# One output-projection unit moved up in a group's first head, and the last logits placed ahead of the last projection's eviction

## What is computed

```python
xn = layernorm(x)
# attention: 32 query heads, 8 key/value heads of 128 channels
q, k, v = xn @ Wq.T, xn @ Wk.T, xn @ Wv.T          # split into heads
q, k = rmsnorm(q, q_norm_w), rmsnorm(k, k_norm_w)
scores = q @ k.T / sqrt(128) + where(rel > 0, -1e30, slope[head] * rel)
out = softmax(scores) @ v
s = out @ Wo.T
# feed-forward with 4-bit style weights (w - zero) * scale
g = silu((silu(xn @ gate) * (xn @ up)) @ down)
result = x + s * g
```

## Time and profile before

| | |
|---|---|
| median of 3 runs | 1325.37 us (1324.14 to 1325.52) |
| the profiled execution | 1325.52 us, of which span of the trace 1323.4 us |
| granted TensorE clock | 0.993 of full speed over the span |
| TensorE busy | 1287.3 us, 97% |
| VectorE busy | 970.1 us, 73% |
| GpSimd busy | 710.2 us, 54% |
| ScalarE busy | 649.8 us, 49% |

### The profile page before, as it was taken

How to read it: one execution, slowest core, us unless ns; L and a number is a source line. 1 busy time by engine, 2 the same in 40 slices (tenths; PEclk the granted TensorE clock), 3 DMA queues, 4 the chain that set the end, 5 groups by cost and what they waited for, 6 DMA issues and landing times. The chain is left out here.

```text
span 1323.4 us, 20983 instructions
## 1 busy us (share of the span) xinstructions
PE 1287.3 (97%) x7138; PEld 1105.0 (83%) x7138; DVE 970.1 (73%) x2072; ACT 649.8 (49%) x1422; POOL 710.2 (54%) x755
## 2 busy tenths in 40 slices
PE   7899999999999999999999999999999989999997
PEld 6778888888888888888888888888888878888886
DVE  4678787778777877787778777877788855555556
ACT  3555565556555555555555555555565523222222
POOL 8645464546455545554555455545555625555553
PEclk8899999999999999999999999999999999999999
DMA  3000000000000000100000000000020036455441
GB/s 121 17 17 17 33 17 17 17 32 17 17 17 32 17 17 17 33 17 17 17 33 17 17 16 33 17 17 17 17 64 20 5 77 194 128 127 127 127 127 64
DMA packets 29468, 57.88 MB, mean 44 GB/s; under 512 B 3648, under 2 KB 3648, under 8 KB 29248
## 3 DMA queue, kind: packets, MB, share of 16 engines
q1 hardware_dynamic: 29232, 56.16, 14.9%
q10 hardware_dynamic: 144, 0.52, 0.1%
HBM read 54.57 MB, written 2.10 MB: 43 GB/s over the span
## 5 line engine op out<-in xcount | busy, mean ns | idle before, releaser
L396 POOL TENSOR_TENSOR pb<-rel,coef 128x1024 f32<-128x1024 f32 (+7 forms) x256 | 293.7, 1162 | 123.9 <-PE T L907 118.1
L497 ACT ACTIVATE pb<-pb,low 128x1024 f32<-128x1024 f32 (+7 forms) x256 | 198.9, 777 | 188.6 <-DVE low L687 186.9
L487 ACT ACTIVATE pt_h<-T 128x512 fp32r<-128x512 f32 (+3 forms) x384 | 185.9, 486 | 115.0 <-PE T L907 111.6
L671 DVE TENSOR_TENSOR pt_l<-T,pt_h 128x512 fp32r<-128x512 f32 (+3 forms) x384 | 210.4, 551 | 41.2 <-ACT pt_h L487 41.1
L687 DVE CUSTOM_DVE_ANT_0 pb<-S,pb,ninv 128x1024 f32<-128x1024 f32 (+7 forms) x256 | 207.8, 812 | 40.7 <-PE S L929 35.8
L907 PE MATMUL T<-ident,pb 128*128 128x128 f32 x1152 | 190.7, 275 | 14.9 <-DVE pb L696 8.4
L907 PEld LDWEIGHTS T<-ident,pb 128*128 128x128 f32 x1152 | 141.6, 141 | 53.6 <-issue 14.0
L696 DVE TENSOR_SCALAR pb<-pb,rinv 128x1024 f32<-128x1024 f32 (+7 forms) x256 | 172.5, 674 | 9.0
L926 PE MATMUL S<-kT_h,q_h 128*128 128x512 f32 (+2 forms) x384 | 142.0, 370 | 0.0
L945 PE MATMUL O<-pt_h,v_h 128*128 128x512 f32 (+2 forms) x384 | 140.7, 366 | 1.0 <-DVE pt_l L671 1.0
L373 POOL TENSOR_TENSOR inv<-ms,cst 128x4 f32<-128x4 f32 x64 | 76.2, 1191 | 120.8 <-DVE ms L719 120.8
(11 more groups left out here) (148 smaller groups left out, 2898.7 us busy)
## 6 DMA issues: line engine op xcount, KB each, us to landing
wq_in<-in_wq SPq DMA_DIRECT2D x32, 256.0 KB, 2.8
wo_in<-in_wo SPq DMA_DIRECT2D x32, 256.0 KB, 2.6
stage<-in_wkv SPq DMA_DIRECT2D x7, 512.0 KB, 3.9
stage<-in_gate_w SPq DMA_DIRECT2D x14, 256.0 KB, 2.6
stage<-in_gate_z SPq DMA_DIRECT2D x14, 256.0 KB, 3.6
stage<-in_gate_s SPq DMA_DIRECT2D x14, 256.0 KB, 5.2
stage<-in_up_w SPq DMA_DIRECT2D x14, 256.0 KB, 5.3
stage<-in_up_z SPq DMA_DIRECT2D x14, 256.0 KB, 6.4
```

Source lines behind the costliest of these rows:

```text
L396: g_.tensor_tensor(pbuf(idx, t), rel[:, TOK - w:TOK], coef[:, t:t + 1].to_broadcast([P, w]), ALU.mult).then_inc(bias_ready, 1)
L487: a_.activation(pt_lot(pt_h, t, n), bank[:, 0:m * P].rearrange("p (k w) -> p k w", w=P), ACT.Copy).then_inc(tr_hi, 1)
L497: a_.activation(pbuf(idx, t), pbuf(idx, t), ACT.Exp, bias=low[:, idx:idx + 1], scale=-1.0, accum_out=rsum[:, idx:idx + 1]).then_inc(exps_r ...
L671: v_.tensor_tensor(pt_lot(pt_l, t, n), bank[:, 0:m * P].rearrange("p (k w) -> p k w", w=P), f(pt_lot(pt_h, t, n)), ALU.subtract).then_inc( ...
```

## The change

Two things, both only in the order of work; no instruction is added or taken away.

1. In the first head of groups 1 to 7, unit `w1_0` is made right behind scores 0 and scores 1, ahead of `v0_0`, and no longer between lots (6,0) and (6,1). Its eviction on DVE moves from behind the `pt_l` of lot (6,0) to behind the second normalise, ahead of `v0_0`'s low part. The wait that belongs to it now asks for all evictions up to the head before's `v1_3`.
2. In every head that has units, DVE takes the logits of the last tile (idx 7) before the eviction of `w3`, no longer after it.

```diff
@@ group_order
-        out += [f"qc0_{j}"] + [f"v0_{j}"] * prev + [f"w0_{j}", f"w1_{j}"] * w
+        if j == 0 and not first:
+            out += ["qc0_0", "w1_0", "v0_0", "w0_0"]
+        else:
+            out += [f"qc0_{j}"] + [f"v0_{j}"] * prev + [f"w0_{j}", f"w1_{j}"] * w
@@ vector, group
                 normalise(h, 1)
+                early = j == 0 and kind != "first"
+                if early:
+                    project(at, f"w1_{j}", unit + 1)
                 if prev:
                     v_lo(at, f"v0_{j}", (j - 1) % PER)
...
                 lot(h, 6, 0)
-                if w:
+                if w and not early:
                     project(at, f"w1_{j}", unit + 1, kind == "first")
                 lot(h, 6, 1)
...
                 v_lo(at, f"v1_{j}", j)
+                logits(h, 7)
                 if w:
                     project(at, f"w3_{j}", unit + 3, kind == "first")
-                logits(h, 7)
@@ tensor, group
                     project(at, f"w{n}_{j}", 4 * (j % 2) + n, h - 2 - j % 2, 0 if j >= 2 else 2,
-                            at.n(f"v0_{j - j % 2}"))
+                            at.a - 1 if early and n == 1 else at.n(f"v0_{j - j % 2}"))
...
                 if j == 0:
                     scores(h, 1)
+                if early:
+                    w_unit(1)
...
                 w_unit(0)
                 lot(h, 6, 0)
-                w_unit(1)
+                if not early:
+                    w_unit(1)
                 lot(h, 6, 1)
```

More of the change, by code:

```diff
@@ L1049, in group, with w_unit @@
                 prev = not (kind == "first" and j == 0)
-                def w_unit(n, h=h, j=j):
+                early = j == 0 and kind != "first"
+                def w_unit(n, h=h, j=j, early=early):
                     if kind == "first" and j < 2:
```

## The result

The changed kernel takes 1330.62 us (median of 6 runs, 1330.4 to 1331.82), the kernel before 1325.07 us in the runs beside it (1324.08 to 1325.52). The ratio is 1.0047 with a 95% interval from 1.0037 to 1.0058: slower by 5.55 us between the medians. The forecast was 1330.5, in a range from 1328 to 1334.7.

A forecast was written before the change was run, and what follows sets the result against it. TensorE, busy 97% of the span, was taken as the bound, with DVE as full in the first heads. 1325.4 + 5.1 (4.7 for groups 1 to 6, 0.4 for group 7, edit 2 nothing) = 1330.5 us, range 1328 to 1334.7.

The forecast's parts named there:

- The stall and what it is worth: TensorE before tile 7's T's, first heads of groups 1 to 7: 0.72 us a group, 5.0 us at most.
- Step A: DVE in front of ssum: the squares come late, so DVE idles 0.74 us and everything behind is late.
- Step B: On DVE, w1_0's eviction, 0.60 us, now stands in front of v0_0's low part and every pt_l.
- The three waits: New TensorE waits for DVE in front of w0_0 (0.58 us), lot (6,1) (0.4) and lot (5,0) (0.70).
- the two rivals in which DVE's lag does not reach it: At lot (5,0): intended gain alone, 1320.4 us, chance 0.07; only the wait at w0_0 counts, 1324.4 us, chance 0.08.
- The sum for a group: TensorE leaves lot (5,0) 0.79 us later in each of groups 1 to 6, 4.7 us in all.
- Group 7: The 0.40 us bracket before tile 3's T's takes up part of the lag; 0.4 us taken as remaining.
- The rule against the trace: Second normalise after the squares falls into POOL's power; the skill's exclusion rule was set aside and nothing added.
- the rival at 1334.7: The normalise waits for POOL's power to end, up to 0.6 us more in each of 7 groups; chance 0.10.
- step C: Named only in the experiments: scores 2 come later and the moved unit no longer covers the chain to lot (5,0).
- third place: Lot (5,0) on TensorE: needs the pt_l of lot (6,0), starts at 314.53, new wait 0.70 us.

The follow-up runs named there:

- e6: Kernel before, with three of w1_0's six matmuls and the squares' transposes ahead of v0_0, which takes qc0_0's output tile, in early heads; 1320.98 us, ratio 0.9974.
- e4: Changed kernel with the squares' transposes of a group's first head behind v0_0's third matmul, not its ninth; 1326.56 us, ratio 1.0013.
- e3: Changed kernel with w1_0's eviction in the first head of groups 1 to 7 cut from 512 to 8 columns; 1327.58 us, ratio 1.0024.
- e5: Changed kernel with the squares' transposes behind v0_0's third matmul and w1_0's eviction cut to 8 columns; 1324.93 us, ratio 1.0004.
- e1: Changed kernel with the last logits put back behind w3's eviction, leaving only the move of w1_0 and its eviction; 1330.41 us, ratio 1.0045.
- e8: From e6: all of w1_0 but 32 columns of its last matmul goes ahead of v0_0, eviction stays late; 1324.63 us, ratio 1.0001 to before.

## Why the prediction was right, point by point

**The stall and what it is worth.** Right. The bracket is gone in all seven heads. "7 x 0.72 = 5.0 us is the most that edit 1 can win" was never tested by itself; e6 wins 0.40 a group of it.

**Step A**, DVE idle 0.74 in front of `ssum`. The bracket is 0.66, and e4, which removes it, wins 0.73. The distance from squares to `ssum` was read as 0.64 and is 307.02 - 306.38 = 0.64. Counted from the k transposes `ssum` comes 10.19 us after and came 9.41 before, 0.78 later where the prediction had 0.74.

**Step B**, 0.60 for the eviction. From 308.61 to 309.21 it is 0.60; e3 removes 0.53 of it and wins 0.55.

**The three waits.** All at their place, for the reasons given. Predicted 0.58, 0.4 and 0.70; the first and the last have brackets of 0.51 and 0.52. That column counts from the modelled end of the last matmul and not from when the next could have started, so it reads less than the delay. In distances of starts the first is 309.02 to 310.04, 1.02 against 0.35 without a wait (e5, 438.69 to 439.04), and the last 313.11 to 314.10, 0.99 against 0.30 (before, 313.44 to 313.74). The three are then 0.67, about 0.25 and 0.69. Lot (5,0) starts 314.10 - 306.38 = 7.72 us behind the squares, where 7.62 was forecast and less than 7 would have been wrong; with that the two rivals in which DVE's lag does not reach it fall.

**The sum for a group.** Mis-sized: 0.79 predicted, 0.95 measured. The chain on DVE was right to 0.01: `ssum` to the `pt_l` of lot (6,0) is 313.27 - 307.02 = 6.25, and the prediction had 5.64 + 0.60. What was missing:

- The step from DVE's end to TensorE's start. I took 0.06, from the normalise and the T's behind it. Behind a low part it is 0.15: 309.21 + 0.68 = 309.89 to 310.04 at `w0_0`. At lot (5,0) that adds 0.09. It could have been read before: in the earlier trace rows the low part ends at 309.08 and `w0_0` starts at 309.23, a wait of a few hundredths that shows no bracket.
- From the k transposes to the squares it is 9.55 after (296.83 to 306.38) and 8.12 before (297.40 to 305.52), 1.43 more where I had 1.39 for the unit: 0.04.
- T's behind a wait take 0.38 to the next row (314.10 to 314.48) and 0.35 without one: 0.03.

0.79 + 0.09 + 0.04 + 0.03 = 0.95. The kinds of wait were right; the step mis-sized most is the one from DVE to TensorE.

**Group 7.** Wrong. I let 0.4 of the lag fall into the bracket in front of tile 3's T's. It is still there:

```profile
978.96 0.63 PE L913 MATMUL T<-ident,pb 128*128 128x128 f32 x4 [0.43 <-DVE pt_l L674]
```

and what holds it is seen in DVE's row for the logits of idx 4 in that head:

```profile
975.43 0.75 DVE L690 CUSTOM_DVE_ANT_0 pb<-S,pb,ninv 128x512 f32<-128x512 f32 x1 [1.12 <-PE S L935]
```

DVE waits there for TensorE's own scores, so the chain in front of the bracket moves with TensorE and the bracket keeps its size. I had taken the work in front of it as held by something else without a row for it. Counted from group 7's k transposes, lot (5,0) is 0.89 later than before and tile 3's T's are 0.78 later: about 0.1 is given back there, not 0.4. From those k transposes to the last `v0_0` it is 125.17 us before, 126.20 in the changed kernel and 125.97 in e1, without edit 2. So of the 1.0 us more, 0.8 is edit 1, where I had 0.4, and 0.2 is edit 2.

**Why the number came out so close.** 5.1 predicted, 5.55 between the medians, some 6.7 by the periods. The forecast was counted from 1325.4, a median that lies in the upper of the two clusters of before. Four of the six times beside the changed kernel lie nearer to that cluster too, while four of the six runs of the changed kernel have the higher mean clock (0.995 to 0.996). Counted between like executions, before is at about 1323.8 and the forecast's own sum would have given 1328.9, where the changed kernel takes 1330.5. The mechanism and its place are shown; that the total came within 0.1 us is luck.

**Edit 2.** Costed at nothing, measured nothing in groups 1 to 6. The idle time in front of the last normalise is gone, as forecast, but only because it has moved in front of the logits, which wait for their scores; the normalise got 0.1 of the 0.2 it was to gain, and lost that by taking longer. Where I allowed up to 0.5 of gain in single heads, group 7 shows a loss of 0.2 in one. TensorE's last T of head 29, which waits for the normalise, changed kernel:

```profile
1020.11 0.33 PE L913 MATMUL T<-ident,pb 128*128 128x128 f32 x1 [0.80 <-DVE pb L699]
```

and e1, without edit 2:

```profile
1019.79 0.33 PE L913 MATMUL T<-ident,pb 128*128 128x128 f32 x1 [0.59 <-DVE pb L699]
```

**The rule against the trace.** The normalise fell into POOL's power as foreseen, and it was not held up. POOL's row:

```profile
312.20 1.19 POOL L376 TENSOR_TENSOR inv<-ms,cst 128x4 f32<-128x4 f32 x1
```

The normalise started at 312.73, not quite half-way through, and took its 0.62. The rule of the Trainium skill ("SBUF — State Buffer", section "Who interferes with whom") that such a pair shuts each other out for the whole instruction did not hold for this power of 128x4 elements, and the rival at 1334.7 fell with it. The two are not free of each other, though: it is the power that grew. It takes 1.01 us where no normalise runs (as at 291.67, for k), and here 1.19, ending at 313.39, just behind the normalise's end at 313.35; in the earlier trace rows it takes 1.18 and ends at 56.71 behind 56.67; in the earlier trace rows, where the normalise began before it, 1.39. GpSimd stands idle for 0.40 us soon after (in front of 314.38, waiting for ACT), so this made nothing later. For a large GpSimd instruction this trace agrees with the rule that the normalise is held up: at 298.29 one of 128 columns, under the biases, took 0.80, against 0.29 in the other heads of a steady group.

```profile
298.29 0.80 DVE L699 TENSOR_SCALAR pb<-pb,rinv 128x128 f32<-128x128 f32 x1
```

**What the argument left out** is step C. The prediction had it hidden in its third place (TensorE is at lot (5,0) sooner, with no unit to cover the chain) and charged all of that wait to DVE's lag of 1.34. e5 and e8 show that with the lag gone the wait is there all the same, most of it because scores 2 are late and some 0.1 because a normalise takes longer there. The forecast did not suffer, since in the changed kernel A and B were the longer path. A reader who had used it to repair the kernel, by A and B alone, would have got e5: no gain.

## What to carry to other kernels

Filling a stall with work from further on has three prices: what the filler delays for the other engine (here the squares), what its result asks of that engine earlier (the eviction), and the hole where it came from, which may have been cover for another chain. Take no more filler than the stall is long: with the squares early and the eviction late in both, three matmuls gained 0.40 us a group (e6) and nearly six lost 0.07 (e8). With the squares late and the eviction early as well, six lost 0.95. Where TensorE's list has no idle time, a delay is never given back, so count it once for each time round.

## What was not expected of the hardware

- From DVE to a TensorE that already waits it takes 0.15 us from the recorded end of a low part to the start of the matmul (309.89 to 310.04), against 0.06 behind a normalise.
- TensorE's granted clock fell to 0.50 (1.2 GHz) for up to some 6 us in group 0, in some executions of a kernel and not in others, and that alone moves the total by about 1.5 us, as much as a whole experiment here. Comparing the same stretch in both traces (here the period of a group) takes it out.
- A normalise of 768 columns that begins half-way through GpSimd's power of 128x4 elements takes its usual 0.62, and the power is what gets longer, 1.19 in place of 1.01, until the normalise has ended.
